# Order of the loads and place of the row normalization in the symmetric product of a graph and mixture-of-experts kernel

## The reference, cut to what matters

```python
def adjacent_mat(adj):
    adj = adj + jnp.eye(adj.shape[0], dtype=adj.dtype)
    deg = jnp.sum(adj, axis=1)
    dinv = jnp.where(deg > 0, deg ** (-0.5), 0.0).astype(adj.dtype)
    return dinv[:, None] * adj * dinv[None, :]

def _L1_gnn_ref(x, Coefficient2, A):
    adj = adjacent_mat((A + A.T) * 0.5)
    y = Coefficient2 @ adj
    return y @ x

x = x + _L1_gnn_ref(_layernorm(x, axis=-1), adj, adj)
```

## Time and profile before

| | us |
|---|---|
| median of 3 runs | 2196.76 |
| lowest and highest of them | 2195.17 and 2202.2 |
| profiled execution, its own time | 2201.98 |
| its span in the trace | 2200.2 |
| the stage `symmetric_product` in it, from its first DMA to its last accumulator read | 1120.7 to 1273.6 |

### The profile page before, as it was taken

How to read it: one execution, slowest core, us unless ns; L and a number is a source line. 1 busy time by engine, 2 the same in 40 slices (tenths; PEclk the granted TensorE clock), 3 DMA queues, 4 the chain that set the end, 5 groups by cost and what they waited for, 6 DMA issues and landing times. The chain is left out here.

```text
span 2200.2 us, 38541 instructions
## 1 busy us (share of the span) xinstructions
PE 1950.8 (89%) x15937; PEld 1714.8 (78%) x15941; DVE 1280.7 (58%) x1732; ACT 1101.2 (50%) x1182; POOL 468.4 (21%) x335
## 2 busy tenths in 40 slices
PE   4869999999987169999948979949999999999998
PEld 4859999999965069999936857638888888888886
DVE  7799988888656347777758033533434334344342
ACT  4699888886934135555412033224435344253441
POOL 2033222211120422222225401262101011011011
PEclk9979999999989679999979989969999999999999
DMA  6443333323202558888757322253334344353432
GB/s 249 155 164 122 117 108 122 117 83 31 98 6 77 196 183 252 250 250 250 186 168 257 122 77 77 75 150 121 103 119 133 98 134 128 106 138 93 125 104 109
DMA packets 154248, 300.01 MB, mean 136 GB/s; under 512 B 16091, under 2 KB 53083, under 8 KB 149968
## 3 DMA queue, kind: packets, MB, share of 16 engines
q1 hardware_dynamic: 135792, 262.30, 36.9%
q0 software_dynamic: 18336, 35.98, 7.7%
HBM read 227.23 MB, written 79.71 MB: 140 GB/s over the span
## 5 line engine op out<-in xcount | busy, mean ns | idle before, releaser
L823 PE MATMUL attn_acc<-heads_vals,gat_adj 128*128 128x99 bf16 x2048 | 284.6, 209 | 0.0
L2093 DVE TENSOR_TENSOR moe_w_lo<-moe_raw,moe_w_hi 128x2048 fp32r<-128x2048 f32 x64 | 146.8, 2293 | 234.6 <-ACT moe_w_hi L2050 234.6
L821 PE MATMUL attn_acc<-heads_vals,one_x 128*128 128x99 bf16 (+1 forms) x2048 | 240.9, 231 | 18.6 <-DVE one_x L735 13.2
L821 PE MATMUL attn_acc<-heads_vals,heads_mask 128*128 128x99 bf16 (+1 forms) x2048 | 238.5, 229 | 0.0
L2050 ACT CAST moe_w_hi<-moe_raw 128x2048 fp32r<-128x2048 f32 x64 | 122.2, 1909 | 207.8 <-PE moe_y_ps L2018 192.6
L688 ACT ACTIVATE heads_mask<-gat_s_row,heads_big_s 128x2048 fp8e4<-128x2048 f32 x104 | 197.8, 1989 | 35.3 <-PE attn_acc L823 35.3
L821 PEld LDWEIGHTS attn_acc<-heads_vals,one_x 128*128 128x128 fp8e4 x2048 | 197.9, 99 | 15.7 <-issue 15.3
L823 PE MATMUL attn_acc<-heads_vals,attn_below 128*128 128x99 bf16 x2048 | 204.9, 212 | 5.3 <-issue 5.3
L688 ACT ACTIVATE one_x<-gat_s_row,heads_big_s 128x2048 fp8e4<-128x2048 f32 x101 | 192.1, 1989 | 23.5 <-PE attn_acc L823 23.5
L821 PEld LDWEIGHTS attn_acc<-heads_vals,heads_mask 128*128 128x128 fp8e4 x2048 | 197.3, 98 | 5.5 <-issue 5.4
L201 PE MATMUL moe_h_ps<-moe_x_hi,moe_w_hi 128*128 128x512 f32 x512 | 200.1, 391 | 1.6 <-DVE moe_x_lo L2098 1.6
(11 more groups left out here) (347 smaller groups left out, 4736.2 us busy)
## 6 DMA issues: line engine op xcount, KB each, us to landing
moe_raw<-in_L_ffn_W_dram SPq DMA_DIRECT2D x64, 1024.0 KB, 5.2
moe_wg<-in_L_ffn_w_gate_dram SPq DMA_DIRECT2D x23, 768.0 KB, 9.1
moe_wu<-in_L_ffn_w_up_dram SPq DMA_DIRECT2D x23, 768.0 KB, 10.7
moe_wd<-in_L_ffn_w_down_dram SPq DMA_DIRECT2D x23, 768.0 KB, 12.3
gat_s_row<-s_rows SPq DMA_DIRECT2D x16, 1024.0 KB, 6.4
sym_a<-in_adj_dram SPq DMA_DIRECT2D x32, 512.0 KB, 4.3
one_seq<-sent SPq DMA_DIRECT2D x23, 514.0 KB, 3.6
sent<-all_zeros SPq DMA_DIRECT2D x10, 1028.0 KB
```

Source lines behind the costliest of these rows:

```text
L821: mm = pe.matmul(o[:, 0:first], mask[u][:, j, cols], both[:, 0:first], start=(j == 0 and b % 2 == 0), stop=(j == NT - 1), skip_group_check ...
L823: mm = pe.matmul(o[:, 3 * C1:6 * C1], second, both[:, 3 * C1:6 * C1], start=False, stop=(j == NT - 1), skip_group_check=True)
L2093: dve.tensor_tensor(w_lo[n % 2][:], raw[:, n % R], w_hi[n % 2][:], ALU.subtract).then_inc(w_low, 1)
```

## The change

Three things are different in the stage, and nothing outside it.

- Loads: rows 0 and 1 are issued first, then each of the first four adjacency tiles is followed by one row (2 to 5), the fourth also by rows 6 and 7; from tile 4 to tile 11, row j + 4 follows tile j as before. `more` has RM = 8 buffers, so a row waits for the join of the row eight before it.
- `z` is made by ACT, as `Identity(z_scale * x + shift)`, one ACTIVATE for each tile, ahead of that tile's z_hi; the waits for a free `z` buffer go with it. DVE makes no z.
- DVE has one more small instruction for each group, `shift = -mean * z_scale`, and ACT a wait for it (`scaled`).

```diff
-        more = c.sb("more", [P, R, D])
+        RM = 8
+        more = c.sb("more", [P, RM, D])
+        shift = c.sb("shift", [P, NT])
...
                 def row(j):
-                    if j >= R:
-                        sp.wait_ge(joined, j - R + 1)
+                    if j >= RM:
+                        sp.wait_ge(joined, j - RM + 1)
...
-                for j in range(R):
-                    row(j)
+                row(0)
+                row(1)
...
-                        if half == 0 and j + R < NT:
+                        if half == 0 and j < R:
+                            row(2 + j)
+                        if half == 0 and j == R - 1:
+                            row(R + 2)
+                            row(R + 3)
+                        if half == 0 and R <= j < NT - R:
                             row(j + R)
...
-                    for j in members(tiles):
-                        if j >= R:
-                            dve.wait_ge(low, j - R + 1)
-                            dve.wait_ge(kept, j - R + 1)
-                        dve.tensor_scalar(z[:, j % R, :], src[:, j, :], mean[:, j:j + 1], z_scale[:, j:j + 1],
-                                          ALU.subtract, ALU.mult).then_inc(made, 1)
+                    dve.scalar_tensor_tensor(out=shift[:, tiles], in0=mean[:, tiles], scalar=-1.0, in1=z_scale[:, tiles],
+                                             op0=ALU.mult, op1=ALU.mult).then_inc(scaled, 1)
...
+                    act.wait_ge(scaled, g + 1)
                     for j in members(tiles):
+                        if j >= R:
+                            act.wait_ge(low, j - R + 1)
+                            act.wait_ge(kept, j - R + 1)
+                        act.activation(z[:, j % R, :], src[:, j, :], ACT.Identity, bias=shift[:, j:j + 1],
+                                       scale=z_scale[:, j:j + 1]).then_inc(made, 1)
                         act.wait_ge(made, j + 1)
```

More of the change, by code:

```diff
@@ L1480, in symmetric_product @@
         made, high, low, kept = (c.sem(n) for n in ("made", "high", "low", "kept"))
-        joined = c.sem("joined")
+        joined, scaled = c.sem("joined"), c.sem("scaled")
         deg_ready, deg_rooted, dinv_ready, varied, rooted, ch_s = (
@@ L1487, in row @@
                 def row(j):
-                    if j >= R:
-                        sp.wait_ge(joined, j - R + 1)
+                    if j >= RM:
+                        sp.wait_ge(joined, j - RM + 1)
                     sp.dma_start(src[:, j, :], totals[0][j * P:(j + 1) * P, :]).then_inc(row_in[j], 16)
-                    sp.dma_start(more[:, j % R, :], totals[1][j * P:(j + 1) * P, :]).then_inc(row_in[j], 16)
-                for j in range(R):
-                    row(j)
+                    sp.dma_start(more[:, j % RM, :], totals[1][j * P:(j + 1) * P, :]).then_inc(row_in[j], 16)
+                row(0)
+                row(1)
                 for half in range(2):
@@ L1529, in _ @@
                         dve.wait_ge(row_in[j], 32)
-                        dve.tensor_tensor(src[:, j, :], src[:, j, :], more[:, j % R, :], ALU.add).then_inc(joined, 1)
+                        dve.tensor_tensor(src[:, j, :], src[:, j, :], more[:, j % RM, :], ALU.add).then_inc(joined, 1)
                     for j in members(tiles):
```

## The result

The changed kernel takes 2202.07 us (median of 20 runs), the kernel before 2198.01 us in its 20 runs: ratio 1.0021, 95% interval 1.0012 to 1.0029. It is slower by 0.2%, within the 0.3% that the prediction called no change, and inside its range of 2189 to 2206. The single figure was 2198, and 2202.07 lies just above the 2194 to 2202 of the case that had been forecast.

The account below looks back on a forecast made before the run. DVE's chain was taken to bound half 0; groups of 18.6 us against 17.8 and a new stall at tile 12 end it 1.0 us later, so 2196.76 + 1.2 = 2198 us, range 2189 to 2206.

Parts of the forecast that it names:

- the case that had been forecast: Whole kernel: 2194 to 2202 us, within 4.5 us of 2198, chance 0.57.
- the trade behind it: DVE's groups: z leaves DVE but returns as its wait for ACT, saving some of POOL's blocking; 18.6 us against 17.8.
- What bounds half 0: First half of the stage: DVE's chain is the bound, strips are not; 13.0 us of PE's waits, all for z_lo.
- ACT's chain: z, z_hi and `out` on ACT: 1.9 us for each tile against 1.15 before, with z at 0.72.
- The group: Four tiles on DVE: 15.1 us unblocked plus 3.5 of POOL's strips, 18.6 us against 17.8 before.
- The start: PE's first matmul in half 0: at 1130.2 instead of 1132.8, 2.6 us earlier, taken back by the next wait.
- The start of tiles 4 to 7: DVE's join of tile 4: about 1147.7 against 1147.47, longer by shift and ACT's z, less 1.4 for one strip.
- The end: End of half 0: z_lo of tile 12 at 1197.3, PE standing 2.2 us, end at 1213.2, 1.0 us later.
- The loads: Stage's loads: first adjacency tile lands 3 us sooner, rows covered by 5 us; the earlier start is lost to later waits.
- Full relief of DVE: Rival in half 0: ACT's pace doesn't hold DVE back; gain 9 to 14 us, 2183 to 2188 us; chance 0.11.
- The slower rival: ACT's pace becomes the bound in half 0: groups reach 20 us, half ends 5.3 us later, 2202 to 2207; chance 0.15.
- all three shown stalls cost the clock: PE's restarts in half 0: low clock behind each, costing 1.4 to 1.9 us; used to place the end at 1213.2.

Follow-up runs that it names:

- e5: The changed kernel, but ACT makes `out` only after all z and z_hi of a group: ratio 0.9984 to the kernel before, stage 84.1 us.
- e1: The kernel before with only the new order of loads and eight buffers for `more`, z still on DVE: ratio 1.0000, stage 90.2 us.
- e2: The changed kernel with the old loads and four buffers for `more`, so only z on ACT and shift on DVE: ratio 1.0011, stage 93.4 us.
- e6: The changed kernel, but DVE joins and takes statistics of the next group between this group's z_lo: ratio 0.9975 to the kernel before, stage 86.3 us.
- e4: The changed kernel with half strips, half of the product left out: ratio 0.9969 to the kernel before, stage 80.6 us, a strip 1.10 us.

## Why the prediction was right, point by point

The call of no change beyond 0.3% and the trade behind it held. The size of the net effect didn't: the stage was forecast 1.0 us longer and became 4.5 us longer, of which the rest of the kernel gave back 0.9 in the profiled execution. Against the kernel before, the whole was forecast 1.2 us longer and is 4.1 us longer. The range was wide enough for that; the trade as forecast, 2194 to 2202, just missed the 2202.07.

**What bounds half 0.** DVE's chain, as said: all of PE's waits are for z_lo, in each kernel that was run but for the first start where the loads are the old ones.

**ACT's chain.** Forecast 1.9 us for a tile with z at 0.72; measured 1.98 with z at 0.81. The term was 4% short, through z alone. The estimate from the Trainium skill (ScalarE: Activation LUTs, What ACT_TABLE_LOAD costs), 0.08 us more for the second pointer, was the better number: the trace has 0.80 to 0.81 with two pointers and 0.72 with one.

**The group.** 15.1 us unblocked and 3.5 of strips were forecast, 18.6 in all. Measured are 18.1, 18.9 and 19.0; with z at 0.81 the unblocked group is 15.4, so strips took 2.7, 3.5 and 3.6. That is the term on which the forecast rested, and e5 shows that ACT's pace is in it. That the 3.5 of strips was met so closely is in part luck: in the second trace the same kernel has a group of 20.8.

**The start.** PE's first matmul was forecast at 1130.2, 9.5 us after the first DMA; it came at 1131.39, after 10.8, since strip 0, begun at 1128.60, blocked the first z_lo. That case had been named, with the z_lo at 1130.5; it ended at 1131.15, so it was priced 0.65 us too low and left out of the sum.

**The start of tiles 4 to 7, the term that was mis-sized.** Forecast 1147.7, measured 1149.91. I had added 1.7 us for shift and ACT and taken 1.4 us of one strip off. In fact shift and ACT took 2.2 us, and strips on DVE did not become less: they took 5.9 us ahead of the join of tile 4, where before they took 5.5. With the loads moved up POOL had begun six strips by then, before only five, the fifth 0.1 us ahead of the join. Strip 0 cost 1.4 us on the first z_lo, and strip 4 cost 1.8 on a 128x2 product. The sum moved by 2.2 us, half of the 4.4. This late start goes with the loads and not with z: the join of tile 4 begins 29.7 us after the first DMA in e1, 29.3 and 28.8 in the two traces of the changed kernel, but 27.2 in e2 and 26.8 and 26.5 in the kernel before.

**The end.** z_lo of tile 12 was forecast at 1197.3 within 3 us, and came at 1199.24 + 0.89 = 1200.1, 2.8 us later than before. In this pair of traces 2.4 of the 2.8 are the late start of tile 4: the two groups between took 37.0 us and 36.9 before. The stall ahead of it, forecast 2.2 us, was 2.78 and cost some clock (granted 0.66 in the 4 us behind it). PE's waits, forecast at some 15 us, were 17.7. Half 0 ended 4.4 us later and not 1.0: 2.8 for that z_lo and 1.6 for the clock behind its stall.

**The loads.** Forecast as neutral, with rows in time and strips not waited for: DVE stood 0.2 us for a row, no strip was waited for, and e1 gives 1.0000. That they advance PE's start was right (10.8 us from the first DMA, 12.1 before). That the strips they advance fall on DVE's first tiles I saw only for strip 0, and counted one strip less instead. Neutral is so true of the whole, by e1, and not of the first four tiles.

**The rivals.** Full relief of DVE did not happen, and e5 and e6 show why: it needs ACT's chain short or DVE's waits filled. The Trainium skill (Perfetto Trace Analysis, Optimizing Scalar/DVE Operations) says that moving work from a saturated DVE to ScalarE may make sense. Taken as a rule it would have the time fall, and the measurement decides against it here (1.0021), as the moved step stood in a loop whose next step waits for it. The slower rival was nearer to the truth than its chance of 0.15 says: groups reached its 19 us, z_lo of tile 12 came 1 us ahead of its 1201.1, and 2202.07 is the lower edge of its 2202 to 2207.

## What to carry to other kernels

Work that is moved to an idler engine takes its place in that engine's order: count the whole loop there between two results that someone waits for, dependent steps with their full duration, before counting what the busy engine saves. What isn't needed soon (`out` here) goes behind what is waited for; that one loop decided between 0.1 to 0.2% lost and 0.12 to 0.16% gained. And where two engines block each other, a chain with short free gaps can fall in step with the engine that blocks it, so judge by the sum over several groups and by two traces, not by one group.

## What the runs showed of the hardware

- A small instruction of one SBUF source can be blocked by a strip or not: the 128x4 TENSOR_SCALAR at 1155.23 took 1.97 us beside the strip of 1155.16, while in the kernel before the 128x1 form of the same line took 0.15 beside a strip that had begun 0.3 us earlier. In e1 the 128x4 form took 1.74 us, with a strip begun at 1150.50 ahead of it at 1150.79. The line's 0.17 was what I had counted.
- shift, with two SBUF sources, is exposed too. In the second trace of the changed kernel, time-line of DVE:

```profile
1197.71 1.94 DVE L1552 SCALAR_TENSOR_TENSOR sym_shift<-sym_mean,sym_z_scale 128x4 f32<-128x4 f32 x1
```

  It took 1.94 us instead of 0.16, beside a strip of 2.00 us that had begun at 1197.63. By the rule of the Trainium skill (SBUF — State Buffer, Who interferes with whom) that instructions of two SBUF inputs contend with GpSimd's reads, this was to be expected, and the trace agrees.
- PE's stalls have a few fixed lengths, since PE itself starts the strip that holds it up. At the end of a tile PE frees the strip's buffer, POOL builds the next strip, and if DVE is then in the z_lo that PE needs, that z_lo ends 0.5 us behind the strip. For tile 12 after the change, time-lines of POOL and DVE (PE ended tile 11 at 1197.50):

```profile
1197.58 2.01 POOL L1518 TENSOR_TENSOR sym_s<-sym_a,sym_at 128x1024 fp32r<-128x1024 f32 x1 [1.61 <-PE sym_acc L1595]
```

```profile
1199.24 0.89 DVE L1556 TENSOR_TENSOR diffuse_z_lo<-sym_z,diffuse_z_hi 128x512 fp32r<-128x512 f32 x1 [1.53 <-ACT diffuse_z_hi L1579]
```

  The wait is 0.08 + 2.01 + 0.54 + 0.15 = 2.78 us. The same 2.78 stands in nine of the fourteen traces. In e4, where a strip takes 1.10 us, the wait of this kind (for tile 12) is 1.87, shorter by the same 0.91 us. The z_lo of tile 12 began 1.66 us behind that strip's start, the z_lo of tile 4 in e5 0.93 us behind its own, and both waits are 2.78. So a z_lo that is ready somewhat sooner or later need not change PE's stall at all.
- Two stalls of PE of the same 2.78 us were followed by different clocks: full after tile 4's, 0.66 in the 4 us after tile 12's. Windows of the changed kernel, columns as in the earlier trace rows:

```profile
1200.20:1204.20 4.00, 3.92 (x12) 3.16 (x13) 1.38 (x2) 3.94 (x7) 0.00 (x0) 0.66 0.53 164
...
1161.50:1165.40 3.90, 3.89 (x17) 3.23 (x18) 1.38 (x2) 3.84 (x7) 0.00 (x0) 1.00 0.86 264
```

  e5 has two stalls of 2.78 us with full clock behind them, e6 two with 0.61 and 0.57; none of the three below 1.9 us in e4 cost clock. From PE's start on tile 12 to the first read of an accumulator it is 13.3 us after the change and in e6, and 11.7 in the second trace of the kernel before, whose stall there was 1.18 us and left the clock full. So the price of a stall of 2.78 us is its length, or its length and 1.6 us; what decides I can't tell from these runs. The forecast's remark that all three shown stalls cost the clock holds for the kernel before (granted 0.57, 0.58 and 0.60 in the 4 us behind them) and not for every stall.
